# Routed experts of a Mamba and mixture-of-experts layer: first weights scaled once and fetched per tile by SyncE's queue, with six result and nine slot buffers and token tiles from group 24

## The chip, the cores and the metric

The kernel runs on one core of a Trainium2 chip. The metric is the device time of the whole program in microseconds (us), the median of several executions. Before the change it is 769.55 us (three executions, 768.49 to 770.16). The engines are named as in the profile: PE (TensorE, matrix products), PEld (its weight loads), DVE (VectorE), ACT (ScalarE), POOL (GpSimd) and SP (SyncE, which here only issues transfers).

## The reference

For 8 sequences of 1024 tokens with 128 channels, two layers follow each other, each with a residual and a layer norm. The first is a Mamba-2 scan (4 heads of 64, state 128), the second a mixture of 14 routed experts, of which each token takes the best 2, and 2 shared ones:

```python
def _ffn(xn, rw, W1, W2):
    ms = jnp.mean(xn * xn, axis=-1, keepdims=True)
    h = xn * jax.lax.rsqrt(ms + RMS_EPS) * rw
    return jax.nn.silu(h @ W1) @ W2
...
gates = jax.nn.softmax(xf @ router_w, axis=-1)
top_v, top_i = jax.lax.top_k(gates, TOP_K)
...
routed = jax.vmap(lambda rw_, W1_, W2_: _ffn(xf, rw_, W1_, W2_))(rms_w, w1, w2)
...
x = _layernorm(x + _L0_attn_ref(x, ...), axis=-1)
x = _layernorm(x + _L0_ffn_ref(x, ...), axis=-1)
```

Each expert has its own vector `rw` of 128 channel weights. It multiplies the expert's input, so a kernel may as well multiply the rows of that expert's W1 (128 x 256) by it.

## The kernel before, in words

All 8192 tokens stay in SBUF, as 64 chunks of 128. One program of 14,716 instructions is written out without loops, and each engine's program is one list that it works through in order, with semaphore waits.

**Main loop.** A Python loop over the steps `i` from -5 to 83 writes the code of all engines; step `i` holds the scan of chunk `i` and later pieces of earlier chunks. Router and ranking follow for every 4 chunks (a token tile of 512 tokens, 16 of them). A ranked token's normalised row is written twice, by POOL's indirect transfers (L669), to the DRAM area `dispatched`, into the region of each expert that it takes. SP's queue, in this loop, loads one block of decays per chunk (L492).

**Routed part.** The regions of the experts are cut into 141 tiles of 128 rows, in 36 groups of 4 (`GROUPS`; the last holds one tile). From step 66 on, groups run beside the last steps, from group 11 on alone. For group `gr`:

- a queue loads 4 slot tiles from `dispatched` into `slots_in` (7 buffers; L451 in `load_slots`): SP's for groups 0 to 15, ACT's from group 16 on, four groups ahead;
- PE turns them (L734), DVE copies the result to `slotsT` (L1426, `turned`);
- DVE multiplies each tile's W1 by that expert's `rms_w` column into one of 8 buffers `w1_now` (L1438, `pick_w1`; the expert's number is in a register); the unscaled W1 of the 14 experts lies in `decay_area`, into which SP's queue loads 1792 KB at group 1, once the scan no longer needs the area;
- PE forms the hidden layer (L745), ACT applies silu (L944), PE forms the output (L770, W2 addressed by a register);
- DVE copies the group's output out of its bank into one of 3 buffers `slots_out` (L1453), and POOL scatters it to the DRAM area `returned` by four indirect transfers (L623, `return_rows`), one per tile.

PE's order in `routed_group(gr)` is: turn group gr+2, hidden layer of gr+1, output of gr. DVE's is: turn copy of gr+2, the four scalings of gr+2, result copy of gr. At group 10 (`FILL_AT`) SP's queue also writes 14 filler blocks behind the ends of the regions (L531).

**Tail.** From group 22 on (`TAIL_FROM` = `LAST_A` 19 + `TAIL_LEAD` 3) each engine does one token tile behind each group, in `by_token`: SP's queue has fetched the tile's two halves from `returned` (`pick`, L500, 5 pairs of buffers), ACT scales one by its gate (L955), DVE adds both to `x` (L1536, L1539) and forms the norm's statistics (L1135, L1139) and, for every second tile, the roots on DVE itself (L1500 to L1521); ACT then normalises (L933) the tile before, for which it waits for those roots, and SP's queue stores it (L504). Fourteen of the sixteen token tiles go beside groups (`TAIL_BESIDE`), the rest follow; the roots of those left are made on POOL (L634, L636).

## Time and profile before

| | |
|---|---|
| median of 3 executions | 769.55 us |
| span of the profiled execution | 769.2 us |
| PE / PEld busy | 651.3 / 554.7 us (85% / 72%) |
| DVE busy | 596.1 us (77%) |
| POOL busy | 501.3 us (65%) |
| ACT busy | 444.7 us (58%) |
| mean granted TensorE clock | 0.926 of full speed |
| DMA | 70.8 MB, mean 92 GB/s |

The span reaches from the first to the last instruction of one execution; what lies around it is the difference of 0.35 us to the median of the timed ones. The busy shares are averages over parts with different limits: the main loop up to about 458 us, in which PE is busy nearly all the time, the routed part, and the tail from 658 us on. So they have to be read by stretch, with the idle times and what ended each. A row of the timeline gives the start (us from the span's start), the duration (us), the engine, the line, the operation and the count of merged instructions, and in brackets the idle time before it with what ended it; "remote" is a semaphore whose sender the profile does not name, "issue" means that nothing visible was waited for.

### The profile page before, as it was taken

The page shows a single profiled execution, that of the slowest core. Times are in us where ns is not written, and L with a number is a line of the kernel's source. Part 1 is how long each engine was busy: PE and PEld are TensorE (multiplying, and loading weights), DVE is VectorE, ACT ScalarE, POOL GpSimd, SP SyncE. Part 2 cuts the span into 40 slices and gives each one's busy share as a digit, 9 for nine tenths or more (in the row PEclk, how much of TensorE's full clock was granted, in tenths as well). Part 3 has the DMA queues.
Part 4 walks back from the last instruction along what each step waited for, and adds up shares of the span by engine and source line. Part 5 has one row for each costly group of instructions (what it writes and reads, how often), then busy time and mean ns, then how long its engine had stood idle before and what let it go on. Part 6 is the DMA issues. An engine that isn't in the chain of part 4 may idle for free.

```text
span 769.2 us, 14716 instructions
## 1 busy us (share of the span) xinstructions
PE 651.3 (85%) x4299; PEld 554.7 (72%) x4299; DVE 596.1 (77%) x1744; ACT 444.7 (58%) x1225; POOL 501.3 (65%) x545
## 2 busy tenths in 40 slices
PE   5987798999999999999999997965988878767830
PEld 4765576788888888888888886854987768656720
DVE  4999999999999999999999864427447343698875
ACT  4885688867877876787787543411223111346445
POOL 1144565887797897888888776556655656566561
PEclk9999999999999999999999998878889889997865
DMA  8541111211221121111111055114222236536126
GB/s 305 193 138 42 43 43 41 64 57 55 62 64 62 60 62 50 63 64 60 59 50 62 22 167 192 45 55 101 80 80 77 76 80 172 168 100 205 60 80 218
DMA packets 62638, 70.76 MB, mean 92 GB/s; under 512 B 10335, under 2 KB 45285, under 8 KB 62304
## 3 DMA queue, kind: packets, MB, share of 16 engines
q1 hardware_dynamic: 41568, 47.70, 19.6%
q0 software_dynamic: 8608, 16.87, 6.5%
q10 hardware_dynamic: 12384, 5.26, 2.9%
q8 instruction: 36, 0.59, 0.3%
q14 instruction: 42, 0.34, 0.1%
HBM read 48.55 MB, written 23.01 MB: 93 GB/s over the span
## 4 chain that ended last, share of the span: by engine, by line
PE 60%; DVE 13%; issue 12%; ACT 7%; another core or an unknown queue 4%; ACTq 2%; DMA 1%; DVEq 0%; SPq 0%
PE bank L745 7%; PE bank L817 6%; PE bank L826 6%; PE bank L884 6%; PE bank L770 5%; PE bank L800 5%; DVE xbcT_area L1155 3%; PE bank L881 3%; PE bank L871 3%; PE bank L833 3%; PE bank L785 3%; PE bank L888 2%; DVE decay_area L1163 2%; ACT x L933 2%
## 5 line engine op out<-in xcount | busy, mean ns | idle before, releaser
L623 POOL DMA_INDIRECT returned<-xT,slots_in x141 | 142.1, 1008 | 107.6 <-DVE xT L1453 67.3
L669 POOL DMA_INDIRECT dispatched<-rows,row_u x128 | 143.7, 1123 | 33.9 <-issue 31.8
L745 PE MATMUL bank<-xT 128*128 128x128 f32 x564 | 92.0, 316 | 43.4 <-issue 24.9
L1155 DVE SCALAR_TENSOR_TENSOR xbcT_area<-raw,conv_w,xbcT_area 128x512 f32<-128x512 f32 x162 | 123.9, 766 | 2.9 <-ACT xbcT_area L999 2.9
L745 PEld LDWEIGHTS bank<-xT 128*128 128x128 f32 x564 | 82.7, 226 | 50.7 <-issue 42.4
L944 ACT ACTIVATE raw<-bank 128x512 f32<-128x512 f32 (+1 forms) x71 | 39.8, 590 | 126.9 <-remote 61.5
L661 POOL TENSOR_TENSOR state_kept<-state,whole 128x256 f32<-128x256 f32 x56 | 72.1, 1288 | 59.0 <-DVE state L1181 49.1
L1453 DVE COPY xT<-bank 128x512 f32<-128x512 f32 (+1 forms) x36 | 24.3, 676 | 90.5 <-remote 72.8
L770 PE MATMUL bank<-xbcT_area,raw 128*128 x564 | 83.4, 308 | 4.7 <-issue 4.6
L1163 DVE TENSOR_TENSOR_SCAN decay_area<-decay_area,ident_heads 128x512 f32<-128x512 f32 x64 | 85.0, 1329 | 0.0
L770 PEld LDWEIGHTS bank<-xbcT_area,raw 128*128 128x128 f32 x564 | 79.6, 224 | 7.0 <-issue 7.0
L970 ACT ACTIVATE zs<-bank 128x256 f32<-128x256 f32 x64 | 24.3, 380 | 96.3 <-PE bank L785 96.3
L933 ACT ACTIVATE x<-x,shift,rstd 128x128 f32<-128x128 f32 x128 | 59.2, 501 | 35.9 <-issue 35.9
L817 PE MATMUL bank<-w_shared,hid 128*128 128x128 f32 x512 | 71.8, 280 | 6.7 <-issue 6.5
L817 PEld LDWEIGHTS bank<-w_shared,hid 128*128 128x128 f32 x512 | 64.7, 196 | 10.0 <-issue 9.8
L826 PE MATMUL bank<-xT,w_shared 128*128 128x512 f32 x128 | 67.6, 608 | 3.0 <-issue 2.5
L884 PE MATMUL bank<-xdt,mix 128*128 128x128 f32 x512 | 67.6, 275 | 0.0
L800 PE MATMUL bank<-xT,w_in 128*128 128x512 f32 x128 | 67.1, 611 | 0.0
L614 POOL TENSOR_TENSOR xend<-xdt,outof 128x256 f32<-128x256 f32 x64 | 63.9, 998 | 0.0
L884 PEld LDWEIGHTS bank<-xdt,mix 128*128 128x128 f32 x512 | 62.3, 192 | 0.0
L1016 ACT ACTIVATE hid<-bank 128x512 f32<-128x512 f32 x64 | 40.4, 631 | 34.1 <-remote 14.9
L979 ACT ACTIVATE xdt<-bank,dt 128x64 f32<-128x64 f32 x256 | 59.5, 316 | 0.3 <-PE bank L792 0.3
(228 smaller groups left out, 1497.0 us busy)
## 6 DMA issues: line engine op xcount, KB each, us to landing
decay_area<-decay_rows SPq DMA_DIRECT2D x64, 256.0 KB
slots_in<-dispatched ACTq DMA_DIRECT2D x77, 64.5 KB
hid<-returned SPq DMA_DIRECT2D x18, 256.0 KB
slots_in<-dispatched SPq DMA_DIRECT2D x64, 64.5 KB
xT<-xT_dram SPq DMA_DIRECT2D x8, 512.0 KB, 7.9
x<-x_dram SPq DMA_DIRECT2D x8, 512.0 KB, 7.8
out_dram<-x SPq DMA_DIRECT2D x16, 256.0 KB
xT<-returned SPq DMA_DIRECT2D x14, 256.0 KB
```

What stands on the lines that cost most here:

```text
L623: e.indirect_dma_start(returned, bass.IndirectOffsetOnAxis(ap=slots_in[sb_][:, n, D:ROW].bitcast(U32), axis=0), slots_out[b][:, n * P:(n + ...
L661: e.tensor_tensor(heads(state_kept[:]), heads(state[(c - 1) % 2][:]), per_head(whole[:, c, :]), ALU.mult).then_inc(S["state_kept"])
L669: e.indirect_dma_start(dispatched, bass.IndirectOffsetOnAxis(ap=row_u[t % 2][:, m:m + 1], axis=0), rows[t % 3][:, k, c4, :], None).then_in ...
L745: mm = e.matmul(bank[:, off:off + P], w1_now[b][:, k * P:(k + 1) * P], slotsT[gr % len(slotsT)][:, n % 4 * P:(n % 4 + 1) * P], start=True, ...
L770: mm = e.matmul(bank[:, j * P:(j + 1) * P], hidden_r[n2 % len(hidden_r)][:, off:off + P], w2_routed[:, bass.ds(experts[4 * (gr % 2) + j], ...
L800: e.matmul(bank[:], w_in[:, DI + k * P:DI + (k + 1) * P], xT[:, t * W:(t + 1) * W], start=True, stop=True).then_inc(S["xbc"])
L817: mm = e.matmul(down_bank[:, c4 * P:(c4 + 1) * P], hid[(4 * t + n) % NHID][:, c4 * P:(c4 + 1) * P], w2_shared[:, e_no, k, :], start=(n == ...
L826: e.matmul(bank[:], w1_shared[:, e_no, k * P:(k + 1) * P], xnT[t], start=True, stop=True).then_inc(S["hidden"])
L884: mm = e.matmul(bank[:, n * P:(n + 1) * P], mix[h][:, k, :], xdt[c % len(xdt)][:, n, zero_first * HD:zero_first * HD + P], start=False, st ...
L933: e.activation(x[:, 4 * t + c, :], x[:, 4 * t + c, :], ACT.Identity, scale=rstd[:, t, 0, c:c + 1], bias=shift[:, t, 0, c:c + 1]).then_inc( ...
L1155: e.scalar_tensor_tensor(o, r[:, n:n + W], conv_w[:, k, TAPS - 1 - n:TAPS - n], o, ALU.mult, ALU.add).then_inc(S["conv"])
L1163: e.tensor_tensor_scan(flat(running[c % 2]), flat(decay_all[b]), flat(ident_heads[:]), 0.0, ALU.mult, ALU.add).then_inc(S["running"])
```

## The change

- W1 of the routed experts is loaded at step 22 of the main loop into an area of its own (`w1_area`, 14,336 bytes of a partition), by SP's queue. ACT multiplies it in place, one expert per step, in steps 24 to 37 (`W1_FROM`), and SP's queue writes the scaled weights to a DRAM area `w1_ready` at step 40.
- The 141 scalings of `pick_w1` on DVE are gone. SP's queue fetches each tile's scaled W1 (128 KB, expert's number in a register) from `w1_ready` into a ring for 3 groups in `decay_area` (`fetch_w1`), for all 36 groups; the fetch of group gr waits until the hidden layer of gr-3 is done.
- `slots_out` has 6 buffers instead of 3, `slots_in` 9 instead of 7; the two new ones lie in `w1_area`.
- `TAIL_LEAD` is 5 instead of 3: token tiles go beside the groups from 24 on, 12 of them, and 4 follow. The first 9 token fetches stay in SP's loop over the groups, 8 groups behind (`PICKS_BEHIND`).
- `dynamic_dma_scratch_size` is set to 2048.

```diff
-    TAIL_LEAD = 3
+    W1_FROM = 24
+    TAIL_LEAD = 5
+    PICKS_BEHIND = 8
...
+    w1_ready = nc.dram_tensor("w1_ready", [P, NR, HB * P], F32, kind="Internal").ap()
...
-        w1_routed = decay_area[:].rearrange("p n h i -> p (n h i)")[:, 0:NR * HB * P].rearrange("p (e f) -> p e f", e=NR)
+        w1_area = sb("w1_area", [P, NR * HB * P])
+        w1_routed = w1_area[:].rearrange("p (e f) -> p e f", e=NR)
+        w1_ring = decay_area[:].rearrange("p n h i -> p (n h i)")[:, 0:3 * 4 * HB * P].rearrange("p (b n f) -> p b n f", b=3, n=4)
...
-        slots_out = [carve(W) for _ in range(3)]
+        slots_out = [carve(W) for _ in range(6)]
         slotsT = [carve(W) for _ in range(3)]
-        w1_now = [carve(HB * P) for _ in range(8)]
...
+                if c == W1_FROM - 2:
+                    e.dma_start(w1_routed, w1_v[:, 0:NR]).then_inc(S["w1r_loaded"], 16)
+                if c == W1_FROM + NR + 2:
+                    on.wait_ge("w1r_scaled", NR)
+                    e.dma_start(w1_ready, w1_routed).then_inc(S["w1r_stored"], 16)
...
+            def fetch_w1(gr, experts):
+
+                b = gr % 3
+                if gr >= 3:
+                    on.wait_ge("routed_hidden", 2 * (gr - 3) + 2)
+                for n in range(len(slot_tiles(gr))):
+                    e.dma_start(w1_ring[:, b, n, :], w1_ready[:, bass.ds(experts[4 * (gr % 2) + n], 1), :].rearrange("p o f -> p (o f)")).then_inc(S[f"w1_in{b}"], 16)
...
-                if gr == 1:
-                    on.wait_ge("mix", NC)
-                    e.dma_start(w1_routed, w1_v[:, 0:NR]).then_inc(S["w1r_loaded"], 16)
+                if gr == 0:
+                    on.wait_ge("w1r_stored", 16)
...
                     load_slots(e, gr, first_rows)
-
-                m = gr - len(slots_in) - LAST_A
+                if gr == 0:
+                    on.wait_ge("mix", NC)
+                if gr % 2 == 0:
+                    w1_experts = experts_of(on, ET.SP, gr)
+                fetch_w1(gr, w1_experts)
+
+                m = gr - PICKS_BEHIND - LAST_A
...
-                    gr, b = n // 4, n % len(w1_now)
-                    on.wait_ge("w1_picked", n + 1)
+                    gr = n // 4
+                    on.wait_ge(f"w1_in{gr % 3}", 16 * tiles_upto(gr, 3))
...
+                if at(i, W1_FROM, NR):
+                    n = i - W1_FROM
+                    on.wait_ge("w1r_loaded", 16)
+                    on.wait_ge("rms_w_loaded", 16)
+                    e.activation(w1_routed[:, n, :], w1_routed[:, n, :], ACT.Copy, scale=rms_w[:, n:n + 1]).then_inc(S["w1r_scaled"])
...
             def next_group(gr):
                 if gr + 2 < GROUPS:
                     turned(gr + 2)
-                    pick_w1(gr + 2)
...
-    nc = bacc.Bacc("TRN2", target_bir_lowering=False, num_devices=1)
+    nc = bacc.Bacc("TRN2", target_bir_lowering=False, num_devices=1, dynamic_dma_scratch_size=2048)
```

On DVE, in the tail, this is what stands between two result copies before: the roots' last instruction, the turn copy (L1426), four times a register step and a scaling (L1438), and the result copy of the next group (L1453).

```order
L1521 SCALAR_TENSOR_TENSOR shift<-mv,rstd 128x4 x2
L1426 COPY xT<-bank4 128x512
L1438 ISA
L1438 TENSOR_SCALAR xT<-decay_area,rms_w 128x256
L1438 ISA
L1438 TENSOR_SCALAR xT<-decay_area,rms_w 128x256
L1438 ISA
L1438 TENSOR_SCALAR xT<-decay_area,rms_w 128x256
L1438 ISA
L1438 TENSOR_SCALAR xT<-decay_area,rms_w 128x256
L1453 COPY xT<-bank5 128x512
L1536 SCALAR_TENSOR_TENSOR x<-hid4,pick_v,x 128x128 x4
```

And now, at the same kind of place of the changed program (its turn copy is L1454, its result copy L1468):

```order
L1536 SCALAR_TENSOR_TENSOR shift<-mv,rstd 128x4 x2
L1454 COPY xT<-bank4 128x512
L1468 COPY xT<-bank5 128x512
L1551 SCALAR_TENSOR_TENSOR x<-hid0,pick_v,x 128x128 x4
L1554 TENSOR_TENSOR x<-x,hid1 128x512
```

The eight rows of L1438 are gone, and nothing has taken their place on DVE.

On SP, around the filler blocks, the slot loads of group 9 (L451, into `slots_in2`) stand before them; the blocks (L531) wait only for the table's first value:

```order
L451 ISA [waits returned2,slotsT]
L451 DMA slots_in2<-dispatched 128x129
L451 ISA
L451 DMA slots_in2<-dispatched 128x129
L451 ISA
L451 DMA slots_in2<-dispatched 128x129
L451 ISA
L451 DMA slots_in2<-dispatched 128x129
L424 TENSOR_LOAD fill_row [waits table,filler_region]
L531 ISA
L531 DMA dispatched<-dispatched 16x1032
```

Now the W1 fetches of group 9 (L527) stand between the slot loads and the blocks (L549 in the changed program), and the first of them waits for the hidden layer of group 6:

```order
L457 DMA slots_in0<-dispatched 128x129
L527 ISA [waits routed_hidden]
L527 DMA decay_area<-w1_ready 128x256
L527 ISA
L527 DMA decay_area<-w1_ready 128x256
L527 ISA
L527 DMA decay_area<-w1_ready 128x256
L527 ISA
L527 DMA decay_area<-w1_ready 128x256
L430 TENSOR_LOAD fill_row [waits table,filler_region]
L549 ISA
L549 DMA dispatched<-dispatched 16x1032
```

So the filler blocks, and the slot loads of group 10 behind them, stand behind a wait for PE that was not there.

## Rows read from the trace of the kernel before

**Rows 1.** Busy time by stretch: us, then PE, PEld, DVE, ACT, POOL, clock, DMA share, GB/s
```profile
200.00:300.00 100.00, 100.00 (x666) 82.67 (x665) 94.26 (x242) 77.11 (x226) 83.40 (x87) 1.00 0.19 61
...
593.00:658.00 65.00, 51.43 (x352) 48.08 (x351) 24.89 (x60) 11.98 (x24) 39.16 (x40) 0.87 0.42 119
...
671.00:734.00 63.00, 44.01 (x310) 41.97 (x309) 54.66 (x238) 32.20 (x86) 35.55 (x34) 0.86 0.42 125
```
**Rows 2.** Waits 592 to 658 us: total us, times, longest
```profile
DVE xT L1453 <- remote: 32.2, 5, 8.3
```
**Rows 3.** Timeline of POOL: first and last scatter of one burst, first of the next
```profile
607.07 0.97 POOL L623 DMA_INDIRECT returned<-xT,slots_in  x1 [3.05 <-DVE xT L1453]
...
616.02 0.97 POOL L623 DMA_INDIRECT returned<-xT,slots_in  x1 [0.30 <-issue]
620.13 0.97 POOL L623 DMA_INDIRECT returned<-xT,slots_in  x1 [3.14 <-DVE xT L1453]
```
**Rows 4.** Timeline of PE and of DVE in the same burst
```profile
611.72 1.95 PE L770 MATMUL bank<-xbcT_area,raw 128*128 x16
...
618.54 0.37 PE L745 MATMUL bank<-xT 128*128 128x128 f32 x1 [1.04 <-issue]
```
```profile
618.67 0.69 DVE L1453 COPY xT<-bank 128x512 f32<-128x512 f32 x1 [7.43 <-remote]
```
**Rows 5.** Timeline of DVE in the tail: copies, scalings and token work of groups 25 to 34
```profile
678.62 0.68 DVE L1453 COPY xT<-bank 128x512 f32<-128x512 f32 x1
681.36 0.69 DVE L1539 TENSOR_TENSOR x<-x,hid 128x512 f32<-128x512 f32 x1 [1.02 <-ACT hid L955]
...
683.81 1.27 DVE L1438 TENSOR_SCALAR xT<-decay_area,rms_w 128x256 f32 x4
685.00 0.68 DVE L1453 COPY xT<-bank 128x512 f32<-128x512 f32 x1
...
691.15 1.16 DVE L1438 TENSOR_SCALAR xT<-decay_area,rms_w 128x256 f32 x4
692.23 0.68 DVE L1453 COPY xT<-bank 128x512 f32<-128x512 f32 x1
...
739.96 0.69 DVE L1453 COPY xT<-bank 128x512 f32<-128x512 f32 x1 [0.50 <-PE bank L770]
```
**Rows 6.** Timeline of ACT: what follows the roots of one token tile
```profile
690.59 0.49 ACT L933 ACTIVATE x<-x,shift,rstd 128x128 f32<-128x128 f32 x1 [5.59 <-issue]
...
692.71 1.09 ACT L944 ACTIVATE raw<-bank 128x512 f32<-128x512 f32 x2 [0.47 <-issue]
```
**Rows 7.** Timeline of SP's queue, the filler blocks, and of ACT's, one group's slots
```profile
521.36 16.20 SPq L531 DMA_DIRECT2D dispatched<-dispatched  x14
```
```profile
606.62 1.82 ACTq L451 DMA_DIRECT2D slots_in<-dispatched  x4
```
**Rows 8.** Timeline of PE: hidden layers of groups 6 and 0, turn of group 10
```profile
537.56 3.16 PE L745 MATMUL bank<-xT 128*128 128x128 f32 x14 [1.74 <-issue]
...
556.40 0.60 PE L734 MATMUL bank<-ident,slots_in 128*128 128x128 f32 x4
```
```profile
464.32 3.64 PE L745 MATMUL bank<-xT 128*128 128x128 f32 x16 [1.40 <-DVE xT L1438]
```
**Rows 9.** The page's group of ACT's silu on 128 x 256
```profile
L970 ACT ACTIVATE zs<-bank 128x256 f32<-128x256 f32 x64 | 24.3, 380 | 96.3 <-PE bank L785 96.3
```
**Rows 10.** Timeline of DVE behind the last group's copy
```profile
748.22 0.28 DVE L1453 COPY xT<-bank 128x128 f32<-128x128 f32 x1
...
755.60 1.13 DVE L1536 SCALAR_TENSOR_TENSOR x<-hid,pick_v,x 128x128 f32<-128x128 f32 x4
...
759.32 1.14 DVE L1536 SCALAR_TENSOR_TENSOR x<-xT,pick_v,x 128x128 f32<-128x128 f32 x4 [0.61 <-DMA xT<-returned]
```
**Rows 11.** Chain of work that ended last: a token fetch of 256 KB
```profile
753.62 5.68 DMA xT<-returned
```
**Rows 12.** The group of L623 between 671 and 734 us: busy us, mean ns
```profile
L623 POOL DMA_INDIRECT returned<-xT,slots_in x34 | 35.5, 1046 | 28.1 <-DVE xT L1453 16.8 <-issue 11.3
```

27 lines of the change are left out of this document (9 added, 18 removed).

## The prediction

> **What bounds the kernel now.** I read the busy time by stretch first, since the shares over the whole span mix three programs. In the main loop PE is busy 100.00 of 100 us, ACT 77.11, with the DMA engines at a share of 0.19 [rows 1]: there a little more ACT work or one more large transfer finds room. Between 593 and 658 us, in the routed part, nobody is full: PE 51.43 of 65, DVE 24.89, POOL 39.16. Between 671 and 734 us, in the tail, DVE is busy 54.66 of 63 [rows 1] and everything else less. So the routed part is bounded by a chain of waits and the tail by DVE.
>
> The waits of the routed part say that DVE's result copy stood 32.2 us in five waits for a "remote" semaphore [rows 2]. The timeline shows one turn of it. POOL scatters two groups, 8 transfers, at 1.28 us from start to start, from 607.07 to 617.0, and starts the next eight at 620.13 [rows 3]: 13.06 us for two groups, 6.53 a group, where POOL alone would need 4 x 1.28 = 5.12. PE had issued the products of the output that is copied at 618.67 already at 611.72 to 613.7, but the copy waited 7.43 us; and in the second half of POOL's burst PE stands still for a microsecond before a single product, with nothing to wait for (1.04 us before 618.54), and the copy is released as that ends [rows 4]. The copy also waits for a result buffer, that of the group three before. The burst holds the two groups just before, so that group's scatters had been issued before 604 (POOL was idle 3.05 us before 607.07) [rows 3]. For the buffer to be the cause they must have taken over 14 us to land. I hold PE, slowed in POOL's burst, to be what the copy waits for. Then six result buffers and two more slot buffers are worth nothing here.
>
> In the tail DVE is the chain: from the copy at 678.62 to that at 692.23, two groups, 13.61 us, it is idle for 1.02 us [rows 5]. From the copy of group 25 at 678.62 to that of group 34 at 739.96 there are nine intervals of 6.82 us.
>
> **The change part by part.** All against the profiled span of 769.2 us; the median lies 0.35 us above it.
>
> W1 ahead of time. 14 ACT instructions on 128 x 256, at 380 ns as the silu of that size [rows 9], are 5.3 us, spread over 14 steps of the main loop in which ACT is idle for 23 of 100 us. The 1792 KB in and out go past SP's decay loads at a DMA share of 0.19 [rows 1], with five decay buffers as cover. I take 0; without the cover 5.3 us.
>
> The first scalings. PE's first hidden layer waited 1.40 us for them and took 3.64 us [rows 8], where 16 products take 1.95 [rows 4]: 3.1 us at most to gain, 0 if the transposed slots are late anyway. I take 1.5.
>
> The middle, groups 1 to 23. Scalings are no longer ahead of PE, but what releases the copies is PE itself. I take 0 and keep the cadence of 13.06 us for two groups; the bound below is rival A.
>
> The filler blocks. They and the slot loads of group 10 now stand behind the fetch of group 9, which waits for group 6's hidden layer. That ended at 537.56 + 3.16 = 540.7 [rows 8]. Then come 4 fetches at 1.82 / 4 = 0.46 us, 1.8 us; 14 blocks, which took 16.20 us in the trace, 1.16 each, but would take 6.4 at ACT's rate [rows 7]; 4 slot loads, 1.8 us; and the landing, which I put at 2 us from 5.68 us for four times the bytes [rows 11]. So the slots of group 10 are there between 552.7 and 562.5, and PE turned them at 556.40 [rows 8]: from 3.7 us of slack to 6.1 us late. I take 2 us lost.
>
> Fetching per tile. 4 transfers of 128 KB a group cost SP 1.8 us of 6.5, and each fetch is released three groups ahead, some 19 us before its use. Behind it in SP's queue stand the token fetches: each is issued after the hidden layer that lies one group ahead of its use. At 5.68 us from issue to landing [rows 11] and 1.8 us for the fetches before it, that is 7.5 us against 6.2 to 6.9: ACT may wait about 1 us for it, beside DVE's work. The DMA engines get 0.5 MB more a group, 85 GB/s on 125, so a share of about 0.7 for 0.42 [rows 1]. I take 0, and up to 1 us a group in rival C.
>
> The tail. Without the scalings (683.81 to 685.00 and 691.15 to 692.23, 2.27 us) and the wait of 1.02 us, DVE needs 13.61 - 3.29 = 10.3 us for two groups [rows 5]. What is late next is the loop through ACT. ACT normalises behind the roots (690.59) and gives silu at 692.71 to 693.8 [rows 6], 3.2 us; PE's half hidden layer and output are 24 products, 2.9 us at 1.95 for 16 [rows 4]; so the copy comes 6.3 us behind the roots, and DVE's turn copy, token work and next roots take 5.5 (685.00 to 691.15, less the turn copy) [rows 5]: 11.8 us for two groups, 5.9 each. But the nearer POOL comes to continuous work the more PE slows, as in the middle, where it gives 6.53 [rows 3]. Between 5.9 and 6.53 I take 6.2: for the ten intervals from group 24 on 10 x (6.82 - 6.2) = 6.2 us gained; bounds 2.9 and 9.2. The copy of group 35 came 748.22 - 739.96 = 8.26 us after that of 34 [rows 5, 10]; now it stands behind one token tile with roots, 692.23 - 685.00 less 1.1, 6.1 us: 2.1 gained.
>
> The end. From the last copy to the end it was 21.0 us. DVE then had one token tile with roots left, and two that waited for the last scatters. Now four stand behind the tile of the last group: 3.1 for that, 2.5 for its roots, 4 x 3.1 = 12.4 (755.60 to 758.7 is one) [rows 10], 18.2 us with the copy. Behind DVE's last tile (759.32 + 3.1 = 762.4) 6.8 us followed, of which some 0.5 is caught up since ACT has less to make good: 24.5 us. That is 3.5 lost; the two tiles fill the idle time before the last fetches and a little more.
>
> Sum: -1.5 + 2.0 - 6.2 - 2.1 + 3.5 = -4.3, so a span of 764.9 and a median of 765.2 us. With the first scalings between 0 and 3.1 gained, the filler blocks between 0 and 6.1 lost and the tail's ten intervals between 2.9 and 9.2 gained, one at its end at a time or two in part, the forecast's own range is 759 to 771.
>
> A rule of the Trainium skill bears on the removed scalings. Scatters took 0.97 us each in the burst of the routed part [rows 3] and 1046 ns in the tail, where DVE is fuller [rows 12]. The page SBUF — State Buffer, section Who interferes with whom, says that DVE's copies and tensor-scalar operations in their two-port modes lock GpSimd out of a shared pair of ports, which also starves the descriptors of its transfers; the trace agrees in sign. By it the tail would gain 34 x 0.076 = 2.6 us of POOL's time at the very most, none of which is in the sum.
>
> **The rivals.**
>
> A. The result buffers are what the copies wait for, and POOL takes over as the bound. For it: the sender of the wait is unnamed. Against it: the 14 us. Then the middle's last 12 groups go at 5.12 instead of 6.53, 17 us, and the tail at 5.9, 9.2 us: -1.5 + 2.0 - 17 - 9.2 - 2.1 + 3.5 = -24.3, a time of 745. Chance 0.12.
>
> B. The tail falls back to the burst cadence: 2.9 instead of 6.2, and the first hidden layer gains nothing. -2.9 - 2.1 + 2.0 + 3.5 = +0.5: 770.0. Chance 0.15.
>
> C. SP's queue becomes the bound, on the other side. Place: groups 10 to 15, where SP issues 8 loads a group. In the trace's block of 14 it needed 1.16 us an issue [rows 7]; at that rate a group takes 9.3 us, 2.8 more than 6.53. It decides from 0.82 us an issue on (6.53 / 8). Three groups until ACT has taken over the slots cost 8.3, the filler blocks 6.1: -1.5 + 6.1 + 8.3 - 8.3 + 3.5 = +8.1, a time of 777.6. Token fetches that are late add to it. Against it: 0.46 us an issue in the quiet stretches. Chance 0.20.
>
> The page SBUF — State Buffer, section The DMA setup-cost knee, speaks for C: a fixed cost of about 2 us per transfer, so that a loop over small tiles runs at a fraction of the rate. By its fit 128 KB take 2.3 us, 9.2 us a group if they came one after another, an estimate; the trace's four loads issued in 1.82 us [rows 7] speak against one after another.
>
> D. The smaller scratch slows POOL's transfers. For it nothing in the trace, since none of its scatters shows a wait of that kind [rows 3]. If POOL lost one transfer's time of 1.28 us a group over 23 groups it would be 29 us, 794. Chance 0.03. The page SBUF — State Buffer, section SBUF size, says that this scratch is the ring of descriptors for GpSimd's transfers, 16 KiB by default; the change leaves an eighth.
>
> **How the numbers follow.** Forecast 0.50, A 0.12, B 0.15, C 0.20, D 0.03. About 0.2% (1.5 us) is what a measurement of this kernel can tell from no change. Faster: 0.44 of the forecast, all of A, 0.04 of B, 0.60. Same: 0.06 and 0.08, 0.14. Slower: 0.03 of B, C and D, 0.26. The range reaches from the forecast's 759 towards A and from 771 to C: 750 to 778, which leaves out A and the upper part of C and D.
>
> **What would show it.** In the changed profile: no row of DVE for scalings of W1; the same bursts of 8 scatters about 13 us apart before the tail, with result copies waiting for "remote" (bursts of 12 or more, or none of these waits, speak for A); PE's turn of group 10 and what ended its wait (a slot load: the filler blocks cost what I said or more); hidden layers that wait for a W1 fetch, or SP issues of over 0.82 us (C); copies of groups 24 to 34 about 6.2 us apart; some 24 us from the last copy to the end. If DVE still waits for nothing in the tail and the copies come 6.8 us apart, the step on the scalings is wrong.

## The result, and the profile after

The changed kernel takes 778.75 us (median of four, 776.19 to 782.29) for 769.02 (four, 768.14 to 770.16): a ratio of 1.0115, with a 95% interval of 1.0085 to 1.0145. The prediction said 765.2, faster. It is slower. The experiments then showed something that no row of one trace could tell: on another chip the same change makes the kernel 1.4% faster. Both are followed below. Ratios leave out two executions that lie hundreds of microseconds above the rest of their kernel, one of b_buffers (1067.56 us) and one of b_ahead (1289.16).

The profiled execution of the changed kernel took 777.74 us with a span of 775.9. Busy time by stretch, columns as in [rows 1]:

```profile
200.00:300.00 100.00, 99.91 (x657) 81.46 (x656) 94.44 (x243) 82.04 (x241) 81.03 (x84) 1.00 0.24 77
593.00:658.00 65.00, 50.80 (x386) 47.43 (x384) 16.00 (x28) 11.10 (x20) 39.02 (x41) 0.95 0.61 177
671.00:734.00 63.00, 48.97 (x329) 45.99 (x328) 40.50 (x167) 29.74 (x78) 36.60 (x36) 0.84 0.78 234
```

DVE's scalings are gone: 16.00 busy us for 24.89 in the middle, 40.50 for 54.66 in the tail. POOL's busy time changes by about 1 us, PE's in the tail grows from 44.01 to 48.97. 14.2 us of DVE's work left the tail and turned into idle time. The waits say for whom, first between 592 and 658 us, then between 671 and 734, and last what the kernel before had there:

```profile
DVE xT L1468 <- remote: 41.5, 6, 9.7
```
```profile
DVE xT L1468 <- remote: 13.1, 5, 6.0
...
DVE xT L1468 <- PE bank L793: 3.9, 3, 1.5
```
```profile
DVE xT L1453 <- remote: 3.7, 2, 2.2
```

The result copy (L1468 now) waits 41.5 us for 32.2 [rows 2], and in the tail 13.1 for 3.7. The timeline of the middle shows the same turn as [rows 3, 4], POOL's first scatter of a burst, its last, the next burst, then PE and the copy:

```profile
613.40 0.99 POOL L646 DMA_INDIRECT returned<-xT,slots_in  x1 [3.20 <-DVE xT L1468]
...
622.36 0.97 POOL L646 DMA_INDIRECT returned<-xT,slots_in  x1 [0.30 <-issue]
626.52 0.97 POOL L646 DMA_INDIRECT returned<-xT,w_area  x1 [3.20 <-DVE xT L1468]
```
```profile
620.59 0.97 PE L768 MATMUL bank<-xT,decay_area 128*128 128x128 f32 x4 [0.74 <-issue]
622.03 0.57 PE L768 MATMUL bank<-xT,decay_area 128*128 128x128 f32 x3 [0.47 <-issue]
623.46 0.40 PE L768 MATMUL bank<-xT,decay_area 128*128 128x128 f32 x2 [0.85 <-issue]
624.89 3.56 PE L793 MATMUL bank<-xbcT_area,raw 128*128 x16 [1.03 <-issue]
```
```profile
625.06 0.69 DVE L1468 COPY xT<-bank 128x512 f32<-128x512 f32 x1 [9.66 <-remote]
```

626.52 - 613.40 = 13.12 us for two groups, as before (13.06), with twice the result buffers and no scaling ahead of PE. In the second half of POOL's burst PE does two to four products every 1.43 us with nothing visible to wait for, and the copy is released as that ends. I call this the standstill. It comes ahead of a fall of the granted clock, to the lower of its two levels. These are the columns of [rows 1] for 618 to 624 us, in the standstill, and for 625 to 628, where the 16 products of the last row take 3.56 us instead of 1.95:

```profile
618.00:624.00 6.00, 3.30 (x21) 2.36 (x19) 0.00 (x0) 1.19 (x2) 4.11 (x5) 1.00 0.29 93
625.00:628.00 3.00, 3.00 (x14) 3.00 (x15) 1.29 (x2) 1.08 (x2) 1.17 (x2) 0.50 0.81 244
```

So PE loses time twice: it stands still at full clock, and then works at half of it.

Cut at DVE's result copies, the traces give this (us; copy n is that of group n; the mark is the start of SP's first slot load, which closes the main loop). Chips of kind 1 (that of series 3, and whichever gave the first runs, for which the record names none) show the standstill, those of kind 2 do not. All rows but the first and the third are experiments told below ("slots ahead": SP's slot loads three groups ahead of its fetches).

| kernel, kind | mark | to copy 0 | 0 to 4 | 4 to 12 | 12 to 22 | 22 to 34 | last copy to end |
|---|---|---|---|---|---|---|---|
| before, 1 | 450.9 | 28.7 | 58.3 | 54.7 | 65.6 | 81.9 | 21.0 |
| before again, 1 | 451.2 | 28.3 | 55.6 | 54.5 | 64.8 | 79.9 | 20.8 |
| changed, 1 | 455.1 | 30.4 | 57.0 | 56.3 | 65.6 | 80.1 | 25.8 |
| slots ahead, 1 | 453.5 | 31.9 | 57.2 | 55.2 | 65.4 | 78.7 | 25.7 |
| slots ahead, lead 4, 1 | 454.9 | 29.9 | 57.1 | 53.8 | 65.1 | 81.7 | 21.9 |
| before with small scratch, 2 | 453.2 | 20.7 | 41.3 | 41.1 | 49.6 | 82.3 | 19.8 |
| six buffers alone, 2 | 452.9 | 21.3 | 41.2 | 40.8 | 40.5 | 90.7 | 20.3 |
| lead 5 alone, 2 | 454.1 | 20.8 | 41.8 | 42.3 | 49.5 | 79.7 | 25.3 |
| changed, 2 | 453.3 | 21.8 | 40.6 | 49.4 | 40.1 | 71.1 | 25.8 |
| slots ahead, 2 | 455.0 | 21.5 | 40.6 | 43.4 | 40.2 | 74.0 | 25.7 |
| slots ahead, lead 4, 2 | 451.7 | 20.6 | 39.9 | 43.3 | 40.2 | 81.7 | 21.8 |

On kind 1, changed less the mean of the two traces of before: mark +4.1, copy 0 +1.9, groups 0 to 4 +0.1, 4 to 12 +1.7, 12 to 22 +0.4, 22 to 34 -0.8, last gap, 34 to 35, -1.6 (5.6 for 8.3 and 6.2), end +4.9; in all +10.7. Against the first trace of before alone it is 6.7, the difference of the spans (775.9 and 769.2): there 0 to 4 is 1.3 shorter, 22 to 34 1.8 and the last gap 2.7.

### The profile page after: what moved, and what is told of

Its sections match the earlier page's. It is cut to its first block, busy times and chain, and to the rows that moved or that the text cites. A ratio compares the mean times of both kernels' runs of the same rounds, so it can differ in the third digit from the quotient of the medians.

```text
span 775.9 us, 14861 instructions
## 1 busy us (share of the span) xinstructions
PE 651.0 (84%) x4299; PEld 553.3 (71%) x4299; DVE 553.6 (71%) x1591; ACT 450.0 (58%) x1239; POOL 498.7 (64%) x547
## 3 DMA queue, kind: packets, MB, share of 16 engines
q1 hardware_dynamic: 62016, 68.03, 28.7%
q10 hardware_dynamic: 12384, 5.26, 2.7%
## 4 chain that ended last, share of the span: by engine, by line
PE 55%; DVE 17%; issue 13%; SPq 5%; ACT 4%; another core or an unknown queue 2%; DMA 2%; ACTq 1%; DVEq 0%
PE bank L849 6%; PE bank L840 6%; PE bank L768 6%; PE bank L907 6%; DVE xbcT_area L1183 5%; PE bank L823 4%; PE bank L793 4%; DVE decay_area L1191 3%; PE bank L904 3%; PE bank L894 3%; PE bank L856 3%; PE bank L808 3%; PE bank L911 2%; PE bank L815 2%
## 5 line engine op out<-in xcount | busy, mean ns | idle before, releaser
L646 POOL DMA_INDIRECT returned<-xT,slots_in x112 | 111.6, 996 | 91.0 <-DVE xT L1468 62.1
L692 POOL DMA_INDIRECT dispatched<-rows,row_u x128 | 143.6, 1122 | 32.2 <-issue 32.2
L1468 DVE COPY xT<-bank 128x512 f32<-128x512 f32 (+1 forms) x36 | 24.5, 680 | 137.6 <-remote 94.3
L768 PE MATMUL bank<-xT,decay_area 128*128 128x128 f32 x564 | 88.0, 305 | 37.6 <-issue 29.5
L768 PEld LDWEIGHTS bank<-xT,decay_area 128*128 128x128 f32 x564 | 79.2, 216 | 45.3 <-issue 40.2
L840 PE MATMUL bank<-w_shared,hid 128*128 128x128 f32 x512 | 69.8, 276 | 5.3 <-issue 5.3
L840 PEld LDWEIGHTS bank<-w_shared,hid 128*128 128x128 f32 x512 | 63.0, 192 | 9.0 <-issue 9.0
L637 POOL TENSOR_TENSOR xend<-xdt,outof 128x256 f32<-128x256 f32 x64 | 66.1, 1032 | 0.0
L907 PEld LDWEIGHTS bank<-xdt,mix 128*128 128x128 f32 x512 | 63.1, 194 | 0.0
## 6 DMA issues: line engine op xcount, KB each, us to landing
slots_in<-dispatched SPq DMA_DIRECT2D x56, 64.5 KB
slots_in<-dispatched ACTq DMA_DIRECT2D x56, 64.5 KB
```

The source lines that it names most:

```text
L637: e.tensor_tensor(xend[h][:].rearrange("p (n s e) -> p n s e", s=2, e=HD), xdt[c % len(xdt)][:].rearrange("p n (s e) -> p n s e", e=HD)[:, ...
L646: e.indirect_dma_start(returned, bass.IndirectOffsetOnAxis(ap=slots_in[sb_][:, n, D:ROW].bitcast(U32), axis=0), slots_out[b][:, n * P:(n + ...
L692: e.indirect_dma_start(dispatched, bass.IndirectOffsetOnAxis(ap=row_u[t % 2][:, m:m + 1], axis=0), rows[t % 3][:, k, c4, :], None).then_in ...
L768: mm = e.matmul(bank[:, off:off + P], w1_ring[:, gr % 3, n % 4, k * P:(k + 1) * P], slotsT[gr % len(slotsT)][:, n % 4 * P:(n % 4 + 1) * P] ...
L840: mm = e.matmul(down_bank[:, c4 * P:(c4 + 1) * P], hid[(4 * t + n) % NHID][:, c4 * P:(c4 + 1) * P], w2_shared[:, e_no, k, :], start=(n == ...
L907: mm = e.matmul(bank[:, n * P:(n + 1) * P], mix[h][:, k, :], xdt[c % len(xdt)][:, n, zero_first * HD:zero_first * HD + P], start=False, st ...
```

## The experiments

Eighteen runs on five chips, fourteen of them kernels not run before; the runs of one series share one chip and their runs of before. Ratios are to before on the same chip. Where an expectation speaks of "the first trace", it is that of before ahead of the prediction.

### Series 1, kind 2: parts of the change alone (before: 719.14 us, 32 runs)

**b_scratch**: `num_devices=1, dynamic_dma_scratch_size=2048` and nothing else.

> The kernel before with one edit, the scratch for POOL's transfers set to 2048. Theory: the scratch never limits its transfers, so the cadence of the scatters (1.28 us from start to start) stays and the time is 769 within 1.5 us. Rival (D of the prediction): POOL waits for free descriptors, the starts move apart, and the time rises by 5 us or more. Second question: what lies around the span was 0.35 us before and is 1.84 us in the changed kernel; if the scratch does that, this kernel shows 1.8 too.

716.54 us, 0.9964 (0.9947 to 0.9981). Rival D falls: scatters start 1.28 us apart as before, and the time is if anything 2.6 us shorter, for which I have no cause. What lies around the span is 1.7 to 1.9 us in every later run of either kernel, so not the scratch's doing; it was 0.35 us in the first runs of before, and 1.5 us of the first 9.7 may be that.

But before takes 719 us here for 769. The kernel is the same, so it is the chip or what held on it then, and a trace of the same kernel on both kinds was needed; see series 3.

**b_buffers**:

```diff
+        slots_in += [carve(4 * ROW).rearrange("p (n w) -> p n w", n=4) for _ in range(2)]
...
-        slots_out = [carve(W) for _ in range(3)]
+        slots_out = [carve(W) for _ in range(6)]
```

> The kernel before with scratch 2048, six result buffers and nine slot buffers, everything else as it was (token fetches issued at the same groups as before). Theory: the copies wait for PE's results, not for a buffer; the waits for a remote semaphore stay (about 70 us in all) and the time is that of the scratch alone within 1.5 us. Rival (A): the buffers were the limit, and the middle groups go faster, 745 to 755 us.

715.7 us, 0.9953 (0.9936 to 0.9969), the same as the scratch alone. Yet the middle is 9 us shorter (40.5 for 49.6). The table shows where it goes: 22 to 34 takes 90.7 for 82.3. DVE's first token work there:

```profile
610.20 1.14 DVE L1539 SCALAR_TENSOR_TENSOR x<-xT,pick_v,x 128x128 f32<-128x128 f32 x4 [12.76 <-DMA xT<-returned]
```

The copies ran ahead of POOL, which still needs 5.12 us a group. The first token tile stands right behind copy 22, as in before. It waits 12.76 us for scatters that POOL has not come to (2.98 in b_scratch). Buffers alone move the wait; they need the later token tiles.

**b_lead5**: `TAIL_LEAD = 5` in before.

> The kernel before with TAIL_LEAD 5 instead of 3 and nothing else: 12 token tiles beside groups, 4 behind them. Theory of the prediction: 2.1 us gained at the last gap, 3.5 lost at the end, so +1.4 and a time of 770.4; from the last result copy to the end 24.5 us for 21.0. Rival from the changed kernel's trace (25.8 us there): the end costs 4.8 and the gap gives less, so 772 to 774.

719.95 us, 1.0012 (0.9997 to 1.0026): +0.8. The end is 25.3 us as the rival had it, for 19.8 in b_scratch. What is won ahead of it nearly pays in the median; the traces show 2.6 us of it, 79.7 for 82.3 from 22 to 34, and not where the rest is.

**b_ahead**: W1 loaded at step 22, 14 scalings on ACT, stored at step 40; the result unused.

> The kernel before with scratch 2048 and, added, the work ahead of time: W1 loaded at step 22, 14 ACT scalings in steps 24 to 37, the scaled weights stored at step 40. Nothing reads them; the routed part scales on DVE as before. Theory of the prediction: hidden, the time is that of the scratch alone within 1.5 us. Rival from the changed kernel's trace (main loop 4.3 us longer, of it 3.0 in two stretches before 130 us in which the granted clock fell to 0.66 and 0.79): the extra work costs 3 to 5 us, 772 to 774. If the two stretches are chance, they are absent here.

717.92 us, 0.9986 (0.9970 to 1.0002), 1.4 us above b_scratch with overlapping intervals. The mark is 453.3 for 453.2. The work ahead is hidden or costs little; the two intervals leave room for up to 3 us.

### Series 2, kind 2 (before: 719.10 us, 17 runs)

**after_again** is the changed kernel.

> The changed kernel once more. The kernel before ran at 769 us beside its first runs and at 719 us on the chip of the last four; there PE never stood still in POOL's bursts and the middle groups went at 4.9 us for 6.5. Theory: the change loses where PE is starved, since its fetches add traffic; where PE is not starved the six result buffers let POOL work without a gap and the ratio to before is 0.985 to 1.00. Rival: the loss has nothing to do with that (main loop, filler blocks, end), and the ratio is 1.01 again.

709.55 us, 0.9860 (0.9838 to 0.9882). The theory holds: the change is 9.5 us faster here. DVE's copies and PE in the middle, one turn of 4.01 us:

```profile
577.06 0.69 DVE L1468 COPY xT<-bank 128x512 f32<-128x512 f32 x1 [2.72 <-PE bank L793]
...
581.07 0.69 DVE L1468 COPY xT<-bank 128x512 f32<-128x512 f32 x1 [2.72 <-PE bank L793]
```
```profile
576.86 0.60 PE L757 MATMUL bank<-ident,slots_in 128*128 128x128 f32 x4
577.30 1.95 PE L768 MATMUL bank<-xT,decay_area 128*128 128x128 f32 x16
579.08 1.95 PE L793 MATMUL bank<-xbcT_area,raw 128*128 x16
580.87 0.60 PE L757 MATMUL bank<-ident,slots_in 128*128 128x128 f32 x4
```

PE is not idle here, at a granted clock of 1.00, the releaser has a name again, and the groups go at PE's own rate. The filler blocks do cost time here, 12.91 us instead of 4.91 from the copy of group 7 to that of group 8:

```profile
523.31 10.34 SPq L549 DMA_DIRECT2D dispatched<-dispatched  x14
534.46 1.89 SPq L457 DMA_DIRECT2D slots_in<-dispatched  x4
```
```profile
538.39 1.11 PE L757 MATMUL bank<-ident,slots_in 128*128 128x128 f32 x4 [4.98 <-DMA slots_in<-dispatched]
```

**a_nofetch**: the fetch only for the groups 0 to 2 (`if gr < 3: fetch_w1(gr, w1_experts)`).

> The changed kernel with the W1 fetches of groups 0 to 2 only; the later groups use the same twelve tiles of weights, so the routed results are others. Theory: the fetches cost time (SP's queue and 18 MB of traffic) and without them it is 5 us or more faster than the changed kernel. Rival (the prediction's step: fetch per tile costs 0): within 1.5 us of the changed kernel.

706.68 us, 0.9829 (0.9805 to 0.9853), 2.9 us faster than the changed kernel, with overlapping intervals. The filler stall is absent from its trace (4 to 12: 41.2 us), since no fetch holds SP's queue. So this kernel cannot tell the fetches' traffic from their place in the queue; behind3_again does.

**b_nopick**: before, scalings for the first two groups only.

> The kernel before with W1 scaled for the first two groups only; the later ones use the same eight scaled tiles, so the routed results are others. No fetch, no scaling, three result buffers, TAIL_LEAD 3. The step of the prediction on the tail: ten intervals fall from 6.82 to about 6.2, 6 us faster than before. Rival: the tail is as fast as POOL, PE and ACT let it, within 1.5 us of before.

714.97 us, 0.9938 (0.9915 to 0.9960), 4.1 us faster. Here the scalings are worth two thirds of the 6.2 us that I took; 22 to 34 takes 78.9 us for 82.3 in b_scratch, and 12 to 22 52.2 for 49.6.

**b_picklate**: `pick_w1(gr + 2)` behind the result copy of gr.

> The kernel before with DVE's four scalings of group gr+2 behind the result copy of gr instead of ahead of it. Theory: in the tail the copy comes 1.2 us earlier and POOL starts earlier, but DVE's work stays the same, so the time is within 1.5 us of before. Rival: the copy is what the chain runs through and the tail gains up to 1 us a group, 5 to 10 us in all.

718.31 us, 0.9996 (0.9976 to 1.0017). Where the scalings stand does not matter, only whether they are there.

### Series 3, kind 1 (before: 765.68 us, 16 runs)

**before_again** is the kernel before.

> The kernel before once more, for its trace on a chip of this series. Theory: PE has no idle time ended by issue between 478 and 650 us (27 us in the first trace), the result copies of groups 6 to 22 come 4.9 us apart for 6.5, and the run takes 719 us. Rival: the 50 us lie in the main loop or the tail.

This chip is of the first kind: 763.07 us. The standstill is there, so what the expectation says of a chip without it could only be tested against series 1. PE's waits from 478 to 650 us, of this kernel and then of b_scratch on kind 2:

```profile
PE bank L770 <- issue: 11.9, 15, 1.1
PE bank L745 <- issue: 10.6, 12, 2.9
PE bank L817 <- issue: 6.9, 12, 1.2
PE bank L734 <- issue: 1.3, 3, 0.5
```
```profile
PE bank L745 <- ACT raw L944: 13.5, 14, 1.7
PE bank L745 <- DVE xT L1438: 10.4, 3, 4.4
PE bank L734 <- DMA slots_in<-dispatched: 2.8, 2, 1.8
```

31.7 us that end with "issue" on the one (1.0 of it in a row not shown), none on the other. The 50 us between the kinds lie between the mark and copy 22, 203.2 us for 152.7. The idle time is only half of that. Between these two points PE is busy 165.07 us on kind 1 and 138.27 on kind 2, with nearly the same products (1143 and 1124 in the trace), and idle 38.1 us for 14.4. The clock granted from the mark to copies 0, 4, 12 and 22 is 0.92, 0.84, 0.92 and 0.89 on kind 1, and 1.00, 0.99, 0.97 and 1.00 on kind 2. So some 24 us are idle time and 27 are the same work done slower, and of that second part the rows above show the order, standstill first and the low clock behind it. It is not the transfers that are slower. POOL's queue, packets, MB and share of the span, before_again (761.3 us) and b_scratch (713.5):

```profile
q0 software_dynamic: 8608, 16.87, 6.6%
```
```profile
q0 software_dynamic: 8608, 16.87, 7.0%
```

That is 50.2 and 49.9 us, and POOL's scatters start 1.28 us apart on both. Each chip was visited once, so what I call the chip's could also be what held on it during its runs; every execution of before on this one took 762 to 769 us.

**a_behind3**: slot loads and filler blocks three groups ahead of the fetches in SP's queue.

```diff
-            for gr in range(GROUPS):
+            for gr in range(GROUPS + 3):
...
                     load_slots(e, gr, first_rows)
+                if gr in (3, 4, 5):
+                    continue
+                gr = gr if gr < 3 else gr - 3
...
                 fetch_w1(gr, w1_experts)
```

> The changed kernel with SyncE's slot loads and filler blocks three groups ahead of the W1 fetches (fetch of group g stands behind the slots of g+3), so that neither waits behind a fetch that waits for PE. Theory: the filler blocks cost the changed kernel 8 us at the copy of group 8 (12.9 us for 4.9), of which POOL, already the bound, lets 3 to 4 arrive at the end, as in the kernel without fetches: ratio 0.980 to 0.984, 706 us. Rival: the fetches' traffic is what the kernel without fetches saved; then the stall goes and the time stays within 1.5 us of the changed kernel's 709.5.

773.92 us, 1.0088 (1.0056 to 1.0120). On this kind the theory's ratio is far off: groups 4 to 12 take 55.2 us for 56.3, so the filler stall was small in these two traces, where the standstill leaves PE late anyway. The kernel stands where the changed one did (1.0115), within the intervals.

**a_behind3_lead4**: also `TAIL_LEAD = 4`, `PICKS_BEHIND = 7`.

> The same with TAIL_LEAD 4 (token tiles from group 23 on, three tiles behind the last group instead of four) and the token fetches one group earlier. Theory: 3.1 us less behind the last copy, but the first token tiles wait for POOL, which is behind the copies by then; net within 2 us of the kernel with lead 5. Rival (the prediction's end term, 3.5 us for two tiles, can be had back alone): 1.7 us or more faster.

771.03 us, 1.0057 (1.0031 to 1.0082). 2.9 us of the loss come back; the end is 21.9 us for 25.7, and 22 to 34 takes 3.0 more.

**a_heavy**: for groups 11 to 33 one more transfer, `e.dma_start(heavy_rows[gr - 11], w1_area[...])`, 1 MB each.

> The changed kernel with one more transfer of 1 MB per group for groups 11 to 33, from SBUF to DRAM on SyncE's queue, that nothing reads; about 150 GB/s more. Question: can traffic alone make PE stand still with nothing visible to wait for, as in the first traces (12 to 16 us before the hidden layers between 478 and 650 us)? Theory: no; PE waits for W1 fetches and slots only, its idle time ended by issue stays under 2 us there, and the time rises by the late fetches. Rival: PE starves, issue waits appear in POOL's bursts.

779.87 us, 1.0201 (1.0165 to 1.0237), 6 us above a_behind3 on the same chip. The 6 us cannot all be put down to the extra traffic. This kernel has the changed kernel's order in SP's queue, and its groups 4 to 12 take 62.4 us for 55.2. SP began its filler blocks at 546.45 and took 13.30 us for them, PE's turn of group 10 stood 5.26 us idle until 564.33, before the first of the extra transfers was issued at 567.46, and the copy of group 8 came 12.95 us behind that of 7, for 7.36 in the changed kernel. That is the filler stall of kind 2 (12.91), so this kind can have it too. From copy 12 to the end it takes 178.7 us, the changed kernel 177.1 and a_behind3 175.5: what the traffic can have cost is 1.6 to 3.2 us.

Between 567 and 650 us, where the extra transfers run (DMA share 0.97, 332 GB/s), PE's idle time ended by issue is 8.6 us, in the changed kernel 13.4 and in a_behind3 16.1; PE waits 9.2 us for slots. More traffic does not make more standstill. Nor does it on kind 2, where PE is busy 48.73 of 50 us at a DMA share of 0.87 (after_again, same columns as above):

```profile
560.00:610.00 50.00, 48.73 (x437) 48.54 (x437) 18.99 (x33) 16.46 (x28) 38.09 (x40) 1.00 0.87 254
```

### Series 4, kind 2 (before: 718.81 us, 11 runs)

**b_pace**: a product of 128 x 256 on POOL ahead of the scatters of groups 11 to 21.

> The kernel before with one product of 128 x 256 on POOL, of about 1 us, which nothing reads, ahead of the four scatters of each group from 11 to 21. Theory: on a chip where PE stands still in POOL's bursts, it does so since more than five scatters stand in a row; with four and a pause the idle time of PE ended by issue between 560 and 650 us goes (27 us in the first trace from 478 on), the copies of groups 12 to 22 come 6.0 to 6.3 us apart for 6.5, and the time falls by 2 to 5 us. Rival: it is the mean rate of scatters; the idle time stays and the time is the same or longer. On a chip without the standstill POOL is the bound and the pause costs 8 to 12 us.

724.27 us, 1.0076 (1.0059 to 1.0092), +5.5 where I said 8 to 12. It came to a chip without the standstill, so whether shorter bursts would end the standstill was not tried.

**a_lead3_3buf**:

```diff
-    TAIL_LEAD = 5
+    TAIL_LEAD = 3
...
-        slots_in += [carve(4 * ROW).rearrange("p (n w) -> p n w", n=4) for _ in range(2)]
...
-        slots_out = [carve(W) for _ in range(6)]
+        slots_out = [carve(W) for _ in range(3)]
```

> The changed kernel with TAIL_LEAD 3, three result buffers and seven slot buffers as before, slot loads three groups ahead of the fetches. What is left of the change is W1 scaled ahead, the fetch per tile and the scratch. Theory: the lead's end term (5 us from last copy to end: 25.6 for 20.8) is what the changed kernel loses on a chip with the standstill; without it the ratio to before is 0.995 to 1.003. Rival: the fetches lose it, and the ratio stays at 1.008 or above. On a chip without the standstill the theory expects 0.990 to 0.997.

723.51 us, 1.0074 (1.0056 to 1.0091): a miss for both. Groups 4 to 12 take 57.7 us. With seven slot buffers a load waits for scatters of seven groups earlier, and behind it in SP's queue stand fetches: PE waited 3.7 us for one. My order made a new wait, so this kernel does not price the fetch.

**a4_nofetch** and **lead4_again**: lead 4 and slots ahead, without and with the fetches of groups 3 to 35.

> The kernel with lead 4 and slots three groups ahead, with the W1 fetches of groups 0 to 2 only; later groups use the same twelve tiles of weights. Theory: the fetches are hidden, within 1.5 us of the kernel with lead 4 beside it. Rival: 3 us or more faster, so the fetches are what the change pays.

> The changed kernel with lead 4 and slots three groups ahead of the fetches, once more, beside the last one on the same chip. On a chip with the standstill 1.003 to 1.008 as measured; on one without, the filler stall of 8 us is gone and two tiles less stand at the end: 0.975 to 0.984, faster than the changed kernel's 0.986.

708.61 us, 0.9865 (0.9843 to 0.9887), and 707.78, 0.9856 (0.9838 to 0.9873). The fetches are hidden: 17 MB cost nothing that can be measured in the whole. In the traces PE does wait 2.6 us for them, and 4 to 12 takes 43.3 us for 40.8; it does not reach the end. Lead 4 is no better here than the changed kernel (0.986): the stall is gone, but 22 to 34 takes 81.7 us for 71.1.

### Series 5, kind 2 (before: 718.85 us, 17 runs)

**b_small**: scatters of 32 rows in groups 11 to 21.

> The kernel before with the scatters of groups 11 to 21 cut to 32 of their 128 rows each; the rows left out keep what 32 transfers of 256 KB, added to SyncE's queue in steps 24 to 39, wrote there. On a chip with the standstill: theory, POOL's descriptor work brings it about; PE's idle time ended by issue goes from 560 us on, and the copies of groups 12 to 22 come 4 to 5 us apart for 6.5, 10 us or more faster. Rival: the number of scatters or something else does it, and they stay at 6.5. On a chip without it: theory, POOL's 5.12 us a group is the bound of the middle with three result buffers; the copies come 4.0 to 4.3 us apart for 4.96, 5 to 9 us, of which the tail may take some back. Rival: DVE's scalings ahead of PE bound it, and the copies stay at 4.9.

718.23 us, 0.9996 (0.9982 to 1.0010). A quarter of the rows hardly shortens a scatter:

```profile
565.91 0.87 POOL L631 DMA_INDIRECT returned<-xT,slots_in  x1 [0.30 <-issue]
567.08 0.87 POOL L631 DMA_INDIRECT returned<-xT,slots_in  x1 [0.30 <-issue]
```

1.17 us from start to start for 1.28, so 12 to 22 falls from 49.6 to 47.7 and POOL stays the bound there. The experiment took away much less than I meant it to. Its total does not price even that: from the last copy to the end it takes 25.8 us for 19.8 in b_scratch, and 5.2 of the 6.0 lie behind the last instruction of any engine (7.7 us to the end of the span, 2.5 in b_scratch), for which I have no cause.

**behind3_again** is a_behind3 on kind 2.

> The changed kernel with SyncE's slot loads and filler blocks three groups ahead of the fetches, lead 5. On a chip without the standstill: theory, the 8 us stall at the copy of group 8 goes, and as in the kernel without fetches 3 us of it arrive, ratio 0.980 to 0.984. Rival: POOL gives back all of it, ratio 0.986 as the changed kernel. On a chip with the standstill: 1.006 to 1.012 as measured.

706.32 us, 0.9825 (0.9799 to 0.9852). The stall is gone (43.4 for 49.4) and about 2.5 us of it reach the end, as in a_nofetch. The theory holds, narrowly (the rival's 0.986 is just outside the interval), and this is the fastest kernel on kind 2, ahead of before and, with intervals that overlap, of the changed one. On kind 1 none of the versions beats before.

## Why the prediction was wrong, step by step

**The middle.** "I take 0 and keep the cadence of 13.06 us": right, 13.12, and 12 to 22 is 65.6 for 65.6. The reason, PE slowed in POOL's bursts, is also right. But I treated it as a property of the program. On four other chips the same program does not show it, and there rival A is what happens: 40.1 for 49.6, faster even than the 5.12 us a group that I priced, since the copies only need PE and POOL catches up later.

**The first scalings**, -1.5, were +1.9. The 3.64 us of [rows 8] were misread: they were not the scalings' doing. The granted clock was 0.50 there (465 to 467 us), and in b_scratch, scalings and all, the same 16 products take 1.95 us at a clock of 1.00. The most that could be gained was the wait of 1.40, not 3.1. In the changed kernel the products ran at 1.00 and took 2.02 us, 13.2 us behind the mark as before (13.4), behind a wait of 2.25. Then PE stood still, once for 5.73 us, and the clock was 0.50 when it went on:

```profile
468.32 2.02 PE L768 MATMUL bank<-xT,decay_area 128*128 128x128 f32 x16 [2.25 <-DVE xT L1454]
...
480.46 2.08 PE L871 MATMUL bank<-router,xT 128*128 128x128 f32 x8 [5.73 <-issue]
```

On kind 2 the stretch to copy 0 is 1.1 us longer than in b_scratch. So the term had no gain in it on either kind.

**The filler blocks**, +2.0 with 6.1 as the bound: +1.7 in the changed kernel on this kind, 8.0 on the other. The block took 13.34 us and PE waited 1.60 us for the slots:

```profile
546.64 13.34 SPq L549 DMA_DIRECT2D dispatched<-dispatched  x14
560.88 2.42 SPq L457 DMA_DIRECT2D slots_in<-dispatched  x4
```
```profile
564.56 0.66 PE L757 MATMUL bank<-ident,slots_in 128*128 128x128 f32 x4 [1.60 <-DMA slots_in<-dispatched]
```

The mechanism was right. The bound was not: I worked it against a PE that is late itself; one that is not late feels it more. And a_heavy, with the same order in SP's queue, shows most of the stall on kind 1, so the 1.7 is partly the luck of one trace.

**The tail is the step that failed.** "For the ten intervals from group 24 on 10 x (6.82 - 6.2) = 6.2 us gained." The ten intervals took 66.9 us, against 68.6 in the first trace of before and 66.9 in the second: between 1.7 gained and nothing. DVE lost its scalings, as planned, and waited for PE instead. My loop had "PE's half hidden layer and output, 24 products, 2.9 us", taken from a place at full clock. In the loop some run at the lower level, and PE is held up ahead of them:

```profile
712.15 1.13 PE L768 MATMUL bank<-xT,decay_area 128*128 128x128 f32 x8 [4.03 <-issue]
714.13 2.08 PE L768 MATMUL bank<-xT,decay_area 128*128 128x128 f32 x8 [0.85 <-ACT raw L967]
716.00 3.62 PE L793 MATMUL bank<-xbcT_area,raw 128*128 x16
```
```profile
719.66 0.69 DVE L1468 COPY xT<-bank 128x512 f32<-128x512 f32 x1 [1.46 <-PE bank L793]
```

Here it is 5.5 us from the first of the last 24 products to the copy's release, not 2.9. The cause of that is the clock, not the scatters beside it. By stretch (columns of [rows 1]), around these products and 14 us earlier:

```profile
700.00:703.00 3.00, 3.00 (x28) 2.81 (x26) 1.80 (x9) 2.89 (x10) 2.39 (x3) 1.00 0.98 283
714.00:720.00 6.00, 5.87 (x27) 5.87 (x28) 2.76 (x11) 5.39 (x16) 3.65 (x4) 0.50 0.58 167
```

At 699.64 to 702.59, also beside scatters, 24 products did take 2.95 us. Of the nine outputs that begin between 679 and 735 us, three ran at the lower level (3.27 to 3.62 us), each of them behind a stretch in which PE had been idle: here 4.03 us. That wait is in the program's order one for DVE: the hidden layer needs the turn copy, which DVE did at 711.33 to 712.01, behind the roots. Nor is a full clock enough. The output that ended at 702.59 was copied at 705.76 after 2.03 us for "remote", 3.2 us late. So the loop of 11.8 us for two groups measured 13.4, and the price of 5.9 a group was wrong by three things that it lacked: the lower clock, PE's wait for the turn copy, and releases that come late. I had named the danger ("the more PE slows") and then took 6.2 between two ends instead of the end that the middle showed, 6.53; even that was low. How the 1.6 us divide among the three is not shown. On kind 2 the same intervals are 63.1 us for 66.3, and there b_nopick, 64.5, shows a gain as well.

**The end**, +3.5, was +4.9 (25.8 for 21.0 and 20.8), and 25.3 for 19.8 with the lead alone on kind 2. Behind the copy DVE's tile of the last group waits 1.56 us for ACT, as it did in before. The sum was built from tiles without that wait, and so lacked it:

```profile
750.13 0.28 DVE L1468 COPY xT<-bank 128x128 f32<-128x128 f32 x1
...
753.02 0.69 DVE L1554 TENSOR_TENSOR x<-x,xT 128x512 f32<-128x512 f32 x1 [1.56 <-ACT xT L978]
```

**The last gap**, -2.1: 5.6 us for 8.3, but the second trace of before has 6.2, so most of the 8.3 was chance of one execution.

**W1 ahead**, 0: the mark is 4.2 us later in the trace. 3.0 of these arise before 130 us, where the changed kernel had not yet done anything new; there the granted clock fell. The first two rows are the changed kernel's, the next two those of before (columns of [rows 1]):

```profile
85.00:90.00 5.00, 5.00 (x23) 3.87 (x22) 5.00 (x10) 1.92 (x8) 3.06 (x4) 0.66 0.01 3
120.00:125.00 5.00, 2.65 (x17) 2.40 (x16) 4.52 (x9) 4.97 (x13) 2.61 (x5) 0.79 0.24 56
```
```profile
85.00:90.00 5.00, 4.92 (x33) 3.87 (x32) 5.00 (x11) 3.89 (x13) 2.45 (x4) 1.00 0.01 2
120.00:125.00 5.00, 4.08 (x25) 3.42 (x26) 5.00 (x11) 3.90 (x14) 3.00 (x3) 1.00 0.15 56
```

The mark of b_lead5, whose main loop is that of before, is 454.1, so one execution may well be that late. Over all traces the mark is 453.5 with the work ahead (mean of eleven) and 452.2 in kernels with the main loop and scratch of before (mean of six), and each of the two sets spreads over 3 us. But b_scratch and b_buffers, with the small scratch and no work ahead, have 453.2 and 452.9. So the 1.4 us may be chance, or the scratch's, or the work's; no run tells them apart.

**The scatters.** POOL's in the tail fell from 1046 ns [rows 12] to 1017 (36 in 36.6 us, in two groups from 671 to 734 us):

```profile
L646 POOL DMA_INDIRECT returned<-xT,slots_in x28 | 28.3, 1012 | 20.9 <-DVE xT L1468 13.0 <-issue 7.9
L646 POOL DMA_INDIRECT returned<-xT,w_area x8 | 8.3, 1031 | 5.2 <-issue 2.7 <-DVE xT L1468 2.5
```

And in the bursts of the middle they stay at 0.97 us with and without scalings. The rule of the Trainium skill (SBUF — State Buffer, Who interferes with whom) has the sign and is worth 1.0 us of POOL's time at most, none of it on the path; before_again had 1036 without any change.

**Rivals.** B was nearest in mechanism (the tail at the burst cadence) but had the end at 3.5 and nothing at the start. C named 777.6, nearly the time, for a reason that did not happen: no hidden layer of the middle has a named wait for a W1 fetch in the changed kernel, a4_nofetch shows them free on kind 2 (on kind 1 no kernel without them was run), and the filler blocks, which C shares with the forecast, cost 1.7. D is excluded.

**What stays open.** What makes PE stand still on kind 1. Shown: it comes in POOL's bursts; it appears on one chip and not on four others with the same program, each visited once; the transfers' own time is the same; more traffic does not add to it; the low clock follows it. Not tried: whether shorter bursts end it, as both kernels made for that ran on kind 2, and whether PE's instructions, rather than its data, come late. And the exact account of the 9.7 us: end 4.9, start 1.9, filler 1.7 and main loop 1.4, less 0.8 in the tail, make 9.1, but only the end is the same in every trace with lead 5. Start and filler rest on few traces (28.3 to 31.9 us to copy 0 in four with the change on kind 1), the main loop's share is the one left open above, and 1.5 may be what lies around the span.

## What to carry to other kernels

Work taken off an engine helps only where that engine is what the loop waits for while everything else runs; price the rest of the loop from rows inside the disturbed stretch, not from a clean one, and look up the granted clock of each row that a price is taken from: 16 products took 1.95 us at 1.00 and 3.6 at 0.50 here. More buffers move the wait to whoever is behind: they paid only together with token tiles that start later, and cost an end of 4.9 us where they did not. An idle time that ends with "issue" in one engine during another's bursts may belong to the chip and not to the program; run the unchanged kernel on a second chip before a forecast rests on it.

## What the runs showed of the hardware

- The same kernel takes 716 to 722 us on four chips, and 762 to 770 in the first runs and series 3. Between mark and copy 22 PE is idle 38.1 us for 14.4 and busy 165.07 for 138.27: it starts a few products every 0.7 or 1.4 us in the later part of POOL's bursts, then works at a granted clock of 0.50 for some microseconds, and semaphores arrive late with it.
- A scatter of 32 rows keeps POOL 0.87 us, one of 128 rows 0.97.
- On kind 2 PE works through a group in 4.01 us beside DMA traffic of 254 GB/s, busy 48.73 of 50 us.
- Executions of one kernel on one chip spread over 5 us (716.4 to 721.8), and the end of the main loop over 3 us between traces. In one trace, that of the changed kernel, the granted clock was below full for a few microseconds around 85 and 120 us.
